# The scales of each batch come from a scratch in DRAM instead of four transposes and a copy

## The chip, the cores and the metric

The kernel runs on one core of one Trainium2 chip. The metric is the device time of one execution in microseconds; the median of three runs of the kernel before is 964.22 us (964.22 to 965.14). The core has TensorE (PE) for matrix products, VectorE (DVE), ScalarE (ACT), GpSimd (POOL), and SyncE (SP), which here issues every DMA.

## What is computed

The input x has 4 batches of 1024 rows of 512. Two layers follow one another, both steered by a vector of 128 numbers per batch (`cond`). Cut to what matters here:

```python
# layer 0, per batch b
scale = cond @ norm_w.T + 1.0                       # (4, 512): a row of 512 scales per batch
h = x * (scale[:, None, :] * rsqrt(mean(x*x) + EPS))
val, gate = split(h @ up_w.T)                       # 512 -> 2 * 2048
h = val * gelu(gate)
y = act_quant(h) @ weight_quant(down_w).T + x
# layer 1, per batch: down and up projection (512 -> 128 -> 512), weights = base + 0.1 * delta(cond)
out = y + relu(y @ Wd_b.T + bd) @ Wu_b.T + bu
```

The `(4, 512)` array `scale` is what the change moves about.

## The kernel before, in words

Each engine runs its own program, and semaphores order them. The 4096 rows are worked in 8 chunks of 512 rows (c = 0 to 7, two per batch), each chunk in 16 steps (j = 0 to 15). In step j PE makes the gate and the value products of one slice of 128 features: 12 matmuls each into a bank of PSUM (`up_products`, L1003 to L1005, f16 in three parts), with ACT's gelu (L565) and DVE's product (L851) behind them. Chunk 0 also prepares the up weights: step j loads (`load_up`), squares on ACT (`w_square`, L524), scales on DVE (`w_exponents`, `w_scale`, L688), transposes on PE (`turn_w`, L980) and splits (ACT `w_hi_half`, L530; DVE `w_lo_half`, L695) the weights that later steps use.

x of the next chunk is prepared during the current one. SP loads it (`load_x`, L277), ACT squares it (`square_x`, L498), POOL makes the reciprocal root, DVE multiplies it by that and by the row of scales (`scale_x`, L713), ACT and DVE split it in two f16 parts, and DMA transposes bring it to the layout that PE wants. For chunk 1 the squares stand in steps 0 and 1 of chunk 0, and `scale_x` in steps 5 and 6; for later chunks in steps 2 to 5 and 8 to 11 of the chunk ahead.

The scales lie on the chip as `sc`, 128 partitions by 4 x 4 (feature k * 128 + p on partition p). `scale_x` needs them along the free axis and the same on all partitions, in `sc_row` (128 x 512). Once a batch this row is made so: PE transposes four broadcast columns of `sc` into the bank TA (`spread_row`, L983 to L987), and ACT copies TA to `sc_row` (`copy_row`, L512 to L516). `row_in` puts both in step 4 of chunk 0 (batch 0) and in step 2 of chunks 1, 3 and 5 (batches 1 to 3). TA is shared with other uses, whose turns are counted by `ta_full` and `ta_freed`.

SP's order is written out by hand: setup loads, `load_up(0)` to `load_up(3)`, the broadcast of bu (L421), `load_x(1)` (L277), then chunk by chunk in `run`. Each `load_up(j)` from 3 on waits until PE has turned the weights whose buffer it takes.

Of the kernel before, what the change touches and what calls it, by code (L numbers as in the profile page):

```python
# [5 lines left out]
F32 = mybir.dt.float32  # L6
# [9 lines left out]
P = 128  # L16
# [7 lines left out]
def conditioned_block(nc, x, cond, norm_w, up_w, down_w, Wd, bd, Wu, bu, Wdd, bdd, Wdu, bdu, out):  # L24
# [15 lines left out]
    xt = x.rearrange("b l d -> (b l) d")  # L40
    ot = out.rearrange("b l d -> (b l) d")
    x1_dram = nc.dram_tensor("x1_scratch", (N, D), F32, kind="Internal").ap()
    delta_dram = nc.dram_tensor("delta_scratch", (GROUPS, P, 512), F32, kind="Internal").ap()
    delta_of = delta_dram.rearrange("g (t q b) (y k m) -> y b (g t) k q m", t=4, q=8, b=NB, y=2, k=2)

# [3 lines left out]
    with ExitStack() as ctx:  # L49
# [3 lines left out]
        def sem(name):  # L53
            return ctx.enter_context(nc.semaphore(name))
# [87 lines left out]
        def piece(p):  # L142
            o = 3072 + (p % 2) * 512
            return qreg[:, o:o + 512]
# [13 lines left out]
        def x_bank(k):  # L158
# [25 lines left out]
        piece_in = [sem(f"piece_in{i}") for i in range(2)]  # L184
        piece_biased, piece_quant, mean_step, base_done = (sem(n) for n in (
            "piece_biased", "piece_quant", "mean_step", "base_done"))
        x0_in = [sem(f"x0_in{t}") for t in range(TT)]
        x_in, x_squared, ms_done, x_rstd, x_scaled = sem("x_in"), sem("x_squared"), sem("ms_done"), sem("x_rstd"), sem("x_scaled")
        ta_full, ta_freed, x_hi_done, x_lo_done, x_turned = (sem(n) for n in (
# [22 lines left out]


        TA_BASE = KD
        TA_SC = TA_BASE + 2
        TA_MEAN = TA_SC + 1
        TA_PIECE = TA_MEAN + 1
        TA0 = TA_PIECE + FT // 2

# [11 lines left out]
            return [t for t, a in enumerate((7, 7, 8, 8) if is_first(c) else (10, 11, 12, 13)) if a == j]  # L231

        def row_in(c, j):
            return c + 1 < NCH and ((is_first(c) and j == 4) or (c % 2 == 1 and j == 2))

        def ta_row(b):
            return TA0 + b - 1 if b else TA_SC

        def mean_slot(c):
            return 1 if is_first(c) else 5  # L240
# [1 line left out]
        def is_first(c):  # L242
            return c == 0
# [27 lines left out]
        def _(sp):  # L271
# [26 lines left out]
            def load_pieces(i):  # L298
                for p in (2 * i, 2 * i + 1):
                    if i == 0 and p == 0:  # L300
                        sp.wait_ge(ta_full, TA_BASE + 2)
                    if i > 0:
                        sp.wait_ge(piece_quant, 4 * (i - 1) + 3 + p % 2)
                    dt, fb = p // 4, p % 4
                    sp.dma_start(piece(p), down_w[dt * P:(dt + 1) * P, fb * 512:(fb + 1) * 512]).then_inc(piece_in[p % 2], 16)

            def load_nat(u):
                m, t = u // 4, u % 4
# [52 lines left out]
            def run(c, par, b):  # L361
                first, last = is_first(c), b is None
                for j in range(FT):
                    if first and j < FT - 4:
                        load_up(j + 4)
                    if not last and not first and j == 1:
                        load_x(c + 1)
                    if not last:
                        for t in turns_in(c, j):
                            turn_x(c + 1, t)  # L370
                    if last and j == 4:
                        sp.wait_ge(x_turned, 32 * TT * c)
                        load_x1(0)
                        sp.wait_ge(val_full, FT * c)
                        load_x1(1)
                    if first and j == 4:
                        load_rows(3)
                        load_pieces(0)
                    if first and 7 <= j < 14:
                        load_pieces(j - 6)  # L380
                    if first and j == 11:
                        for u in range(NAT):
                            load_nat(u)
                    for u in units_at(c, j):
                        if u + NAT < UNITS:
                            load_nat(u + NAT)
                    if not first:
                        if j in (7, 8):
                            load_xr(c - 1, j - 7)
                        if 10 <= j < 10 + TT:  # L390
                            store_x1(c - 1, j - 10)
                        if j in (11, 12):
                            load_xr(c - 1, j - 9)
                    for m in batch_at(c, j):
                        if m % 2 == 1:
                            store_stage(m)
                    if last and j == 6:
                        load_deltas()
# [19 lines left out]
            load_rows(1)  # L418
            load_rows(2)
            load_up(3)  # L420
            sp.dma_start(bu_bc[:, :], bu.rearrange("(a d) -> a d", a=1).to_broadcast([P, D])).then_inc(bu_in, 16)  # L421
            load_x(1)
            chunks(run)
# [67 lines left out]
        def _(act):  # L491
# [17 lines left out]
                    act.wait_ge(x_turned, 32 * TT * (n - 1))  # L509
                act.activation(xn_hi[:, t, :], xn[:, t, :], ACT.Copy).then_inc(x_hi_done, 1)  # L510

            def copy_row(b):  # L512
                act.wait_ge(ta_full, ta_row(b) + 1)
                if b > 0:
                    act.wait_ge(x_scaled, TT * 2 * b)
                act.activation(sc_row[:, :], TA[:, :], ACT.Copy).then_inc(ta_freed, 1)  # L516

            def w_square(jj):
                act.wait_ge(upn_in[jj % 3], 32 * (jj // 3 + 1))
                for i in range(2):  # L520
# [35 lines left out]
            def run(c, par, b):  # L556
                first, last = is_first(c), b is None
                for j in range(FT):
                    n = FT * c + j
                    act.wait_ge(gate_full, n + 1)  # L560
                    if first:
                        act.wait_ge(desc_done, max(1, j - 1))
                    if not (first and j < 2):
                        act.wait_ge(max_done, n - 1)
                    act.activation(g[:, j % 2, :], GATE[j % 2][:, :], ACT.Gelu,  # L565
                                   scale=desc[:, 2 * j + 1:2 * j + 2]).then_inc(gelu_done, 1)
                    if first and j + 2 < FT:
                        w_hi_half(j + 2)
                    if first and j + 3 < FT:
                        w_square(j + 3)  # L570
                    if not first and j == 0:
                        copy_scales(c - 1)
                    if not first and j < 8:
                        round_pair(c - 1, 2 * j)
                    act.wait_ge(h_done, n + 1)
                    act.activation(g[:, j % 2, :], h[:, j, :], ACT.Abs).then_inc(abs_done, 1)  # L576
                    if not last:
                        for t in squares_in(c, j):
                            square_x(c + 1, 1 - par, t)
                        if row_in(c, j):  # L580
                            copy_row(b)
                        for t in scalings_in(c, j):
                            x_high(c + 1, t)
                    if first and 7 <= j < 15:
                        for p in (2 * (j - 7), 2 * (j - 7) + 1):
                            act.wait_ge(piece_in[p % 2], 16 * (p // 2 + 1))
                            if p == 0:
                                act.wait_ge(mean_step, 3)
                            act.activation(piece(p), piece(p), ACT.Copy, scale=wtot[:, 2:3], bias=ROUND).then_inc(piece_biased, 1)
                    if first and j >= 8:  # L590
                        copy_pieces(j - 8)
                    if first and j < 6:
                        for m in {4: (4, 5), 5: (6, 7)}.get(j, (j,)):
                            act.wait_ge(rows_in[m // 2], 16)
                            half = down_rows(m // 2)[:, FF // 2 * (m % 2):FF // 2 * (m % 2 + 1)]
                            act.activation(half, half, ACT.Abs, accum_out=wabs[:, m:m + 1]).then_inc(rows_summed, 1)
                    for m in batch_at(c, j):
                        if m % 2 == 1:
                            read_sums(m)
# [67 lines left out]
        def _(dve):  # L667
# [41 lines left out]
            def scale_x(n, t, b):  # L709
                if t == 0:  # L710
                    dve.wait_ge(x_rstd, n + 1)
                    dve.wait_ge(ta_freed, ta_row(b) + 1)
                dve.scalar_tensor_tensor(xn[:, t, :], xn[:, t, :], rstd[:, t:t + 1], sc_row[:, :],  # L713
                                         ALU.mult, ALU.mult).then_inc(x_scaled, 1)

# [252 lines left out]
        def _(pe):  # L968
# [11 lines left out]
                        mm = pe.transpose(w_bank(jj)[i][:, k * P:(k + 1) * P], upn(jj, i)[:, k * P:(k + 1) * P], identf[:, :])  # L980
                    mm.then_inc(w_turned, 1)

            def spread_row(b):  # L983
                pe.wait_ge(ta_freed, ta_row(b))
                for k in range(KD):
                    mm = pe.transpose(TA[:, k * P:(k + 1) * P], sc[:, k, b:b + 1].to_broadcast([P, P]), identf[:, :])
                mm.then_inc(ta_full, 1)  # L987

            def turn_pieces(i):
                pe.wait_ge(piece_quant, 4 * i + 4)  # L990
                pe.wait_ge(ta_freed, TA_PIECE + i)
# [78 lines left out]
            def run(c, par, b):  # L1070
# [5 lines left out]
                for j in range(FT):  # L1076
# [29 lines left out]
                    up_products(par, j, VAL[j % 2], val_full)  # L1106
                    if not first and j == 0:
                        spread_scales(c - 1)
                    if row_in(c, j):
                        spread_row(b)  # L1110
                    if first and j >= 8:
                        turn_pieces(j - 8)
                    if not first and 9 <= j < 9 + TT:
# [143 lines left out]
```

## Time and profile before

| what | value |
|---|---|
| median of 3 runs | 964.22 us |
| profiled execution: time, span | 964.68 us, 962.8 us |
| granted TensorE clock over the span | 0.995 of full speed |
| PE busy | 945.7 us (98%) |
| DVE busy | 690.6 us (72%) |
| ACT busy | 435.6 us (45%) |
| SP's DMA queue | 48.6% of 16 DMA engines, mean 147 GB/s |

The span runs from the first to the last instruction of the profiled execution; 1.9 us of its time lie outside. Matmuls overlap in their pipeline, so one of PE's durations is longer than its step to the next start, and what an instruction costs on PE is read from the distance of the starts.

### The profile page before, as it was taken

The numbers are of one execution on the slowest core, as the hardware profiler recorded it, in microseconds if no ns is written. First come the engines' busy times: TensorE is split into PE (matmuls) and PEld (weight loads), VectorE is DVE, ScalarE is ACT, GpSimd is POOL, SyncE is SP. The second block draws the span as 40 slices with busy tenths as digits, with TensorE's granted clock in tenths as the row PEclk, the third lists the DMA queues.
The fourth block names the chain that finished last, engine by engine and source line by source line (L and its number), as shares of the span: only waits on it lengthen the run. The fifth ranks groups of instructions, "written<-read, shape, count | busy, mean of one in ns | idle before, by whom it ended". The sixth has DMA issues, their size and how long they took to land.

```text
span 962.8 us, 13718 instructions
## 1 busy us (share of the span) xinstructions
PE 945.7 (98%) x5296; PEld 467.1 (49%) x5296; DVE 690.6 (72%) x1095; ACT 435.6 (45%) x801; POOL 52.7 (5%) x52
## 2 busy tenths in 40 slices
PE   7999999999999999999999999999999999999997
PEld 5555544444444444444444444444444444445585
DVE  5869887875877677866877587866977675256665
ACT  4878757322751257322752156312742256214343
POOL 1000000000000000000000000000000000000564
PEclk9999999999999999999999999999999999999999
DMA  9446543464435642564536743574436641320584
GB/s 331 150 137 165 174 160 99 142 183 124 153 122 154 175 132 98 151 177 122 164 110 164 168 146 92 154 182 118 148 112 182 167 138 55 94 77 23 183 298 175
DMA packets 103770, 141.95 MB, mean 147 GB/s; under 512 B 35732, under 2 KB 41368, under 8 KB 103192
## 3 DMA queue, kind: packets, MB, share of 16 engines
q1 hardware_dynamic: 103704, 141.06, 48.6%
q8 instruction: 42, 0.69, 0.3%
q14 instruction: 24, 0.20, 0.1%
HBM read 112.72 MB, written 20.97 MB: 139 GB/s over the span
## 4 chain that ended last, share of the span: by engine, by line
PE 95%; DVE 2%; ACT 1%; issue 1%; DMA 1%; SPq 0%; DVEq 0%; ACTq 0%
PE bank L1003 23%; PE bank L1004 22%; PE bank L1005 22%; PE bank L1056 10%; PE bank L1015 6%; PE bank L1066 1%; PE bank L980 1%; PE bank L1181 1%; PE bank L1173 1%; PE bank L1212 1%; PE bank L1202 1%; PE bank L1204 1%; PE bank L1213 1%; PE bank L1203 1%; PE bank L1194 1%
## 5 line engine op out<-in xcount | busy, mean ns | idle before, releaser
L1003 PE MATMUL bank<-x_split,w_hi 128*128 128x512 f16 x1024 | 389.4, 380 | 2.3 <-DVE x_split L706 2.3
L1004 PE MATMUL bank<-x_split,w_hi 128*128 128x512 f16 x1024 | 389.0, 380 | 0.0
L1005 PE MATMUL bank<-x_split,w_lo 128*128 128x512 f16 x1024 | 388.8, 380 | 0.0
L754 DVE STREAM_TRANSPOSE delta_reg<-delta_reg 128x512 f32<-128x512 f32 x256 | 261.2, 1111 | 13.1 <-PE bank L1015 13.1
L576 ACT ACTIVATE g<-h 128x512 f32<-128x512 f32 x128 | 80.7, 630 | 272.5 <-DVE h L851 272.5
L851 DVE SCALAR_TENSOR_TENSOR h<-bank,desc,g 128x512 f32<-128x512 f32 x128 | 94.7, 740 | 106.1 <-issue 78.2
L1003 PEld LDWEIGHTS bank<-x_split,w_hi 128*128 128x128 f16 x1024 | 100.5, 98 | 128.0 <-issue 10.6
L565 ACT ACTIVATE g<-bank,desc 128x512 f32<-128x512 f32 x128 | 87.6, 685 | 164.1 <-PE bank L1005 163.9
L1005 PEld LDWEIGHTS bank<-x_split,w_lo 128*128 128x128 f16 x1024 | 100.4, 98 | 121.4 <-issue 1.1
L1004 PEld LDWEIGHTS bank<-x_split,w_hi 128*128 128x128 f16 x1024 | 100.3, 98 | 112.6 <-issue 0.8
L1056 PE MATMUL bank<-wqT,qreg 128*128 128x512 fp8e4 x448 | 101.3, 379 | 0.0
L764 DVE TENSOR_TENSOR absrun<-absrun,g 128x512 f32<-128x512 f32 x120 | 82.5, 687 | 24.5 <-ACT g L576 23.6
L736 DVE TENSOR_TENSOR h<-h,s_bc 128x512 f32<-128x512 f32 x112 | 71.9, 684 | 2.0 <-ACT s_bc L549 2.0
L806 DVE SCALAR_TENSOR_TENSOR xr<-bank,fy,xr 128x512 f32<-128x512 f32 x30 | 22.4, 750 | 66.4 <-DMA xr<-in_x 29.4
L1056 PEld LDWEIGHTS bank<-wqT,qreg 128*128 128x128 bf16 x448 | 43.8, 98 | 52.9
L542 ACT ACTIVATE h<-h 128x512 f32<-128x512 f32 x112 | 64.4, 622 | 5.3 <-DVE h L736 5.3
L545 ACT ACTIVATE qreg<-h 128x512 bf16<-128x512 f32 x112 | 63.6, 616 | 0.0
L1015 PE MATMUL bank<-delta_reg,cond_diag 128*32 128x256 f32 x1024 | 61.9, 382 | 0.0
L464 POOL TENSOR_TENSOR rstd<-ss,mhalf 128x4 f32<-128x4 f32 x8 | 10.7, 1335 | 691.3 <-DVE ss L700 691.3
L1015 PEld LDWEIGHTS bank<-delta_reg,cond_diag 128*32 128x32 f32 x1024 | 30.0, 109 | 30.0 <-issue 13.6
L695 DVE TENSOR_TENSOR w_lo<-bank,w_hi 128x512 f16<-128x512 f32 x32 | 20.6, 685 | 12.1 <-ACT w_hi L530 12.1
L524 ACT ACTIVATE xr<-qreg 128x512 f32<-128x512 f32 x32 | 20.3, 635 | 2.8 <-DMA qreg<-in_L_cond_up_w 2.2
(164 smaller groups left out, 622.3 us busy)
## 6 DMA issues: line engine op xcount, KB each, us to landing
delta_reg<-in_L_cond_Wdd SPq DMA_DIRECT2D x64, 512.0 KB, 3.7
delta_reg<-in_L_cond_Wdu SPq DMA_DIRECT2D x64, 512.0 KB, 3.7
qreg<-in_L_cond_up_w SPq DMA_DIRECT2D x32, 256.0 KB, 4.4
xr<-in_x SPq DMA_DIRECT2D x30, 256.0 KB, 4.0
x_scratch<-xr SPq DMA_DIRECT2D x30, 256.0 KB, 4.5
xn<-in_x SPq DMA_DIRECT2D x7, 1024.0 KB, 6.3
h<-in_L_cond_down_w SPq DMA_DIRECT2D x4, 1024.0 KB, 7.8
qreg<-in_L_cond_down_w SPq DMA_DIRECT2D x16, 256.0 KB, 3.7
```

What stands on the lines that cost most here:

```text
L542: act.activation(h[:, k, :], h[:, k, :], ACT.Copy, bias=ROUND).then_inc(round_added, 1)
L565: act.activation(g[:, j % 2, :], GATE[j % 2][:, :], ACT.Gelu, scale=desc[:, 2 * j + 1:2 * j + 2]).then_inc(gelu_done, 1)
L576: act.activation(g[:, j % 2, :], h[:, j, :], ACT.Abs).then_inc(abs_done, 1)
L736: dve.tensor_tensor(h[:, k, :], h[:, k, :], s_bc[:, :], ALU.mult).then_inc(h_scaled, 1)
L754: last = dve.transpose(natT[:, t, kk, :, :].rearrange("p a (r e) -> p e a r", e=4), nat[:, u % NAT, kk, :])
L764: dve.tensor_tensor(absrun[:, :], absrun[:, :], g[:, j % 2, :], ALU.max).then_inc(max_done, 1)
L851: dve.scalar_tensor_tensor(h[:, j, :], VAL[j % 2][:, :], desc[:, 2 * j:2 * j + 1], g[:, j % 2, :], ALU.mult, ALU.mult).then_inc(h_done, 1)
L1003: pe.matmul(bank[:, :], w_hi[:, k, cols], xh[:, par, k, :], start=(k == 0), stop=False)
L1004: pe.matmul(bank[:, :], w_hi[:, k, cols], xl[:, par, k, :], start=False, stop=False)
L1005: mm = pe.matmul(bank[:, :], w_lo[:, k, cols], xh[:, par, k, :], start=False, stop=(k == KD - 1))
L1015: mm = pe.matmul(HY[32 * t:32 * t + 32, cols], cond_diag[:, a, :], natT[:, (4 * m + t) % NATT, :, a, :], start=(a == 0), stop=(a == HB - 1))
L1056: mm = pe.matmul(Y[:, :], q[:, f, t * P:(t + 1) * P], wqT[:, f, :], start=(f == 0), stop=(f == FT - 1))
```

## The change

The row of scales no longer passes through PE and ACT. In the setup SP writes `sc` to a scratch of 4 x 512 words in DRAM, in four DMAs (one per group of 128 features), each with 128 partitions by 4 single words. Once a batch SP reads one row of 512 words from the scratch, repeated for all 128 partitions, into `sc_row`. The four writes stand between `load_up(3)` and the broadcast of bu; the reads stand in step 3 of chunks 0, 1, 3 and 5. `scale_x` waits for the read in place of the copy, and the turn of TA for the row is gone.

```diff
+    sc_dram = nc.dram_tensor("sc_scratch", (NB, D), F32, kind="Internal").ap()
...
-        TA_SC = TA_BASE + 2
-        TA_MEAN = TA_SC + 1
+        TA_MEAN = TA_BASE + 2
...
         def row_in(c, j):
-            return c + 1 < NCH and ((is_first(c) and j == 4) or (c % 2 == 1 and j == 2))
+            return c + 1 < NCH and ((is_first(c) and j == 3) or (c % 2 == 1 and j == 3))
...
+            def load_row(b):
+                if b == 0:
+                    sp.wait_ge(sc_stored, 16 * KD)
+                else:
+                    sp.wait_ge(x_scaled, TT * 2 * b)
+                sp.dma_start(sc_row[:, :], sc_dram[b:b + 1, :].to_broadcast([P, D])).then_inc(sc_row_in, 16)
...
+                    if row_in(c, j):
+                        load_row(b)
...
             load_up(3)
+            sp.wait_ge(setup_dve, 9)
+            with nc.allow_non_contiguous_dma(reason="2048 words, once"):
+                for k in range(KD):
+                    sp.dma_start(sc_dram[:, k * P:(k + 1) * P].rearrange("b p -> p b"), sc[:, k, :]).then_inc(sc_stored, 16)
             sp.dma_start(bu_bc[:, :], ...)
             load_x(1)
...
-            def copy_row(b):
-                act.wait_ge(ta_full, ta_row(b) + 1)
-                if b > 0:
-                    act.wait_ge(x_scaled, TT * 2 * b)
-                act.activation(sc_row[:, :], TA[:, :], ACT.Copy).then_inc(ta_freed, 1)
...
                 if t == 0:
                     dve.wait_ge(x_rstd, n + 1)
-                    dve.wait_ge(ta_freed, ta_row(b) + 1)
+                    dve.wait_ge(sc_row_in, 16 * (b + 1))
...
-            def spread_row(b):
-                pe.wait_ge(ta_freed, ta_row(b))
-                for k in range(KD):
-                    mm = pe.transpose(TA[:, k * P:(k + 1) * P], sc[:, k, b:b + 1].to_broadcast([P, P]), identf[:, :])
-                mm.then_inc(ta_full, 1)
```

On SP, at the end of the setup, the order before was the following (L291 is `load_up`, L421 the broadcast of bu, L277 `load_x(1)`):

```order
L291 DMA qreg<-in_L_cond_up_w 128x512 x2
L421 DMA bu_bc<-in_L_cond_bu 128x512
L277 DMA xn<-in_x 128x4x512
L291 DMA qreg<-in_L_cond_up_w 128x512 x10
L296 DMA h<-in_L_cond_down_w 128x2048
```

The same place of SP's program now (L289 is `load_up`, L431 the writes to the scratch, L275 `load_x(1)`, L310 the read of the row of batch 0):

```order
L289 DMA qreg<-in_L_cond_up_w 128x512 x2
L431 DMA sc_scratch<-sc 128x4x1 x4
L432 DMA bu_bc<-in_L_cond_bu 128x512
L275 DMA xn<-in_x 128x4x512
L289 DMA qreg<-in_L_cond_up_w 128x512 x8
L310 DMA sc_row<-sc_scratch 128x512
L289 DMA qreg<-in_L_cond_up_w 128x512 x2
L294 DMA h<-in_L_cond_down_w 128x2048
```

Four DMAs of single words have moved in ahead of `load_x(1)`, and the read of the row stands four weight tiles later, behind `load_up(7)`.

On PE, in step 4 of chunk 0, the last value products, the transposes of the row (L986) and the first gate products of step 5 stood so:

```order
L1003 MATMUL bank<-x_split,w_hi 128x512
L1004 MATMUL bank<-x_split,w_hi 128x512
L1005 MATMUL bank<-x_split,w_lo 128x512
L986 MATMUL bank<-identf,sc 128x128 x4
L1003 MATMUL bank<-x_split,w_hi 128x512
L1004 MATMUL bank<-x_split,w_hi 128x512
```

The same place now, where L1000 to L1002 are the same three products:

```order
L1000 MATMUL bank<-x_split,w_hi 128x512
L1001 MATMUL bank<-x_split,w_hi 128x512
L1002 MATMUL bank<-x_split,w_lo 128x512
L1000 MATMUL bank<-x_split,w_hi 128x512
L1001 MATMUL bank<-x_split,w_hi 128x512
```

The products now follow one another; nothing else on PE is moved.

## Rows read from the trace of the kernel before

**Rows 1.** The page: busy time by engine, and the chain that ended last

```profile
PE 945.7 (98%) x5296; PEld 467.1 (49%) x5296; DVE 690.6 (72%) x1095; ACT 435.6 (45%) x801; POOL 52.7 (5%) x52
PE 95%; DVE 2%; ACT 1%; issue 1%; DMA 1%; SPq 0%; DVEq 0%; ACTq 0%
```

**Rows 2.** Timeline of PE in chunk 0: start, us, engine line op out<-in

```profile
51.93 0.38 PE L1005 MATMUL bank<-x_split,w_lo 128*128 128x512 f16 x1
52.15 0.60 PE L986 MATMUL bank<-identf,sc 128*128 128x128 f32 x4
52.58 0.38 PE L1003 MATMUL bank<-x_split,w_hi 128*128 128x512 f16 x1
...
67.06 0.38 PE L1005 MATMUL bank<-x_split,w_lo 128*128 128x512 f16 x1
69.74 1.97 PE L980 MATMUL bank<-identf,qreg 128*128 128x128 f32 x8 [2.30 <-DVE qreg L688]
```

**Rows 3.** Stretches: PE, PEld, DVE, ACT, POOL busy, granted clock, DMA share, GB/s

```profile
65.00:70.00 5.00, 2.70 (x13) 1.15 (x12) 3.43 (x12) 3.88 (x10) 0.00 (x0) 0.95 0.14 33
70.00:75.00 5.00, 5.00 (x23) 3.15 (x23) 4.80 (x12) 4.10 (x9) 0.00 (x0) 0.71 0.19 39
355.00:365.00 10.00, 10.00 (x51) 4.78 (x49) 9.31 (x13) 7.06 (x15) 0.00 (x0) 1.00 0.34 106
```

**Rows 4.** Instructions of L986 and of L516: duration ns min/median/max, first and last start

```profile
L986 PE MATMUL bank<-identf,sc x16: 272/273/273, 52.1 to 575.6; 128*128 128x128 f32 x16
...
L516 ACT ACTIVATE sc_row<-bank x4: 575/577/582, 53.7 to 577.5; 128x512 f32<-128x512 f32 x4
```

**Rows 5.** The chain in order of time, 55 to 75 us

```profile
58.37 0.22 PE bank L1004
58.89 0.75 DVE h L851
```

**Rows 6.** L277: us from issue to landing, min/median/max

```profile
DMA to landing us min/median/max: 5.8/6.3/9.9
```

**Rows 7.** Timeline of DVE: steps 1 and 5 of chunk 0

```profile
32.08 1.29 DVE L695 TENSOR_TENSOR w_lo<-bank,w_hi 128x512 f16<-128x512 f32 x2 [0.81 <-ACT w_hi L530]
33.38 0.75 DVE L851 SCALAR_TENSOR_TENSOR h<-bank,desc,g 128x512 f32<-128x512 f32 x1
34.92 0.88 DVE L688 TENSOR_SCALAR qreg<-qreg,winv 128x512 f32<-128x512 f32 x2
...
61.23 1.41 DVE L713 SCALAR_TENSOR_TENSOR xn<-xn,rstd,sc_row 128x512 f32<-128x512 f32 x2
```

**Rows 8.** Timeline of SP, setup: issues, their start and duration

```profile
9.87 2.80 SPq L417 DMA_DIRECT2D bdc<-in_L_cond_bd  x1
12.71 0.91 SPq L296 DMA_DIRECT2D h<-in_L_cond_down_w  x2
...
17.65 0.43 SPq L277 DMA_DIRECT2D xn<-in_x  x1
```

**Rows 9.** DMA in 14.9:15.9, in 22:27 and in 17:30

```profile
DMA packets 604, 0.35 MB, mean 349 GB/s; under 512 B 21, under 2 KB 571, under 8 KB 604
DMA packets 1004, 1.94 MB, mean 387 GB/s; under 512 B 69, under 2 KB 69, under 8 KB 1002
DMA  9999999999999998999999999999999999999521
```

**Rows 10.** Timeline of ACT, steps 0 and 1 of chunk 0

```profile
28.10 0.63 ACT L576 ACTIVATE g<-h 128x512 f32<-128x512 f32 x1 [0.74 <-DVE h L851]
28.64 0.61 ACT L498 ACTIVATE x_split<-xn 128x512 bf16<-128x512 f32 x1
30.90 0.67 ACT L565 ACTIVATE g<-bank,desc 128x512 f32<-128x512 f32 x1
31.47 1.06 ACT L530 ACTIVATE w_hi<-bank 128x512 f16<-128x512 f32 x2
```

**Rows 11.** Timeline of PE, step 2 of chunk 0

```profile
36.14 1.04 PE L980 MATMUL bank<-identf,qreg 128*128 128x128 f32 x8
```

More of the change, by code:

```diff
@@ L186, in conditioned_block @@
             "piece_biased", "piece_quant", "mean_step", "base_done"))
+        sc_stored, sc_row_in = sem("sc_stored"), sem("sc_row_in")
         x0_in = [sem(f"x0_in{t}") for t in range(TT)]
@@ L233, in row_in @@
         def row_in(c, j):
-            return c + 1 < NCH and ((is_first(c) and j == 4) or (c % 2 == 1 and j == 2))
-        def ta_row(b):
-            return TA0 + b - 1 if b else TA_SC
+            return c + 1 < NCH and ((is_first(c) and j == 3) or (c % 2 == 1 and j == 3))
         def mean_slot(c):
@@ L579, in run @@
                             square_x(c + 1, 1 - par, t)
-                        if row_in(c, j):
-                            copy_row(b)
                         for t in scalings_in(c, j):
@@ L1108, in run @@
                         spread_scales(c - 1)
-                    if row_in(c, j):
-                        spread_row(b)
                     if first and j >= 8:
```

## Prediction

> **What bounds the kernel now.** I read the page's busy times and chain first, then PE's timeline at the removed transposes, then what the new DMAs move: the timelines of SP, ACT, DVE and PE over the first 40 us. PE is busy for 98% of the span and makes 95% of the chain [rows 1], so what leaves PE's queue leaves the time one for one, and what makes PE wait adds one for one. DVE and ACT matter only where PE waits for them, which after the setup is in chunk 0, where they also prepare the weights. The largest such wait there is at 67 us: PE stands for 2.30 us before the weight transposes at 69.74 [rows 2], and the granted clock then falls to 0.71 on average in the next 5 us, a stretch partly at the lower of the two levels, 1.2 GHz [rows 3]. Remember that pair; it gives the price of any stall of that length.
>
> **What is removed.** Sixteen transposes on PE, four per batch [rows 4]. Their durations overlap, so I take the distance of starts: the first of four starts at 52.15, the next matmul at 52.58, 0.43 us later, and the matmul ahead of them stands at 51.93, its usual 0.22 us before [rows 2]. No wait is mixed in. The other three fours have the same duration each (272 to 273 ns) and stand in stretches in which PE is never idle, as the one around the third shows [rows 3]. 4 x 0.43 = 1.7 us leave PE, all on the path.
>
> Four copies of 0.577 us leave ACT [rows 4]. Three stand in chunks where ACT is busy for 7.06 of 10 us and PE waits for nobody [rows 3]: worth nothing. The one of batch 0, at 53.7, stands some 5 us ahead of the chain that ends in the stall at 67 us. In that chain DVE's product starts at 58.89 and the chain comes to it from PE [rows 5], so an earlier ACT does not help by itself; PE is 0.43 us earlier and the chain moves with it. The stall keeps its length and the 1.7 us stand. The wait for a turn of TA goes too; PE never stood at it.
>
> **What is added after the setup.** Four reads of 256 KB. DMA share is 0.34 in such a stretch [rows 3] and each read is used five steps after its issue in chunks 1, 3 and 5 (a step is 962.8 us / 128 = 7.5 us on average, against 6.3 us for a load of 1 MB [rows 6]). SP loses about 0.45 us at each. The first is issued behind `load_up(7)`, near 38 us, and used at 61.23 [rows 7]. All hidden; the cover fails only if the writes to the scratch have not landed by about 50 us, since SP would then stand in front of `load_up(8)`. So four reads: 0.
>
> **What is added in the setup.** Four writes of 128 x 4 words, 512 pieces of 4 bytes each, 2048 in all, or 128 per DMA engine; with one semaphore update for each DMA 132. Their data are ready when SP gets there. They stand ahead of the broadcast of bu and of `load_x(1)`, issued at 17.65 [rows 8], 9.9 us to landing, the longest of its kind [rows 6], so it lands at 27.55. The DMA engines are saturated from 17 us to 29 us [rows 9], so SP's delay is at first free (the queue has work), but the engines' time for 2048 pieces is not.
>
> No row shows a 4-byte write to DRAM. From below: nothing but the four issues, 0.43 us each [rows 8], all inside the backlog, 0 us. From the rows of small reads: with pieces of mostly 512 B, 604 packets take 1 us of 16 engines, 26 ns each; with pieces of mostly 2 KB, 1004 take 5 us, 80 ns each [rows 9]. 132 x 26 ns = 3.4 us; 132 x 80 ns = 10.6 us as the upper end. A 4-byte piece carries far less than 512 B, so I take two thirds of the nearer price, about 2.2 us, and keep 0 and 10.6 us.
>
> The load of x then lands by either of two limits. Queue: 27.55 + 2.2 = 29.8. Issue: the four writes put 2112 more pieces in a queue that already held SP at its issues (2.80 us for one of 128 words, against 0.43 [rows 8]), so SP probably comes past them only when the queue has reached them. Before, it reached the 1 MB of x at 27.55 less 1.05 MB / 387 GB/s = 24.8 us, and the 256 KB of bu ahead of it at 24.1. I estimate that `load_x(1)` is issued near 24 us instead of 17.65; with the shortest landing time, 5.8 us [rows 6], that is 29.8 too. I take 29.9.
>
> Who waits: ACT's first square of chunk 1 starts at 28.64, directly behind its L576 [rows 10]. Behind it in ACT's queue are another square, a sum of the down weights, gelu of step 1 (30.90), the upper halves of weight tile 3 (31.47) and the squares of tile 4. None of these shows idle time ahead [rows 10], so a late landing moves them all. DVE's `w_lo` at 32.08 waits for ACT, its product at 33.38 follows at once, and the scaling of tile 4 starts at 34.92 [rows 7] and ends its first half near 35.4. PE turns this half at 36.14 [rows 11]: slack about 0.75 us. So PE stands by (landing - 28.64 - 0.75) = landing - 29.4. At 29.9 this is 0.5 us. Until step 5 ACT and DVE find their lost time again, since their idle gaps in steps 2 to 4 are waits for PE.
>
> The sum: -1.7 + 0.5 = -1.2 us. Against the profiled execution, 964.68 us, that is 963.5; the profiled run stands 0.46 us above the median of the runs, 964.22, so against the median I get 963.0 us.
>
> The Trainium skill has a rule against this change: in "DMA: Bandwidth & Descriptors", section "Rules for kernel authors", a strided last dimension becomes one descriptor per element, and its "Specifications" say that below 512 B the DMA engine does a read-modify-write. The only single-word DMA here is a read (the issue of 2.80 us), so no run shows the second; if it doubles the price of each piece, the rival below is the outcome.
>
> **The rivals.** (0.2% of this kernel is 1.9 us, about what a measurement can tell from no change.)
>
> A. All hidden: the writes cost the engines under about 1.5 us and x lands before 29.4. Then the full 1.7 us stay: 962.5. For it: 4 bytes are almost nothing, and the queue is backlogged anyway. Against it: the shortest landing after a late issue is already 29.8. Even this is 0.18%, just inside no change.
>
> B. Late x, slower. If x(1) lands after about 31.7 us, PE stands for over 2.3 us at the transposes of 36.14, as long as the stall after which the clock fell [rows 2], and what follows runs at the lower level. In the stretch 70 to 75 the clock was 0.71, so 0.29 x 5 = 1.45 us were missing, and about 0.2 us in the stretch before: 1.7 us. Two ways lead here. The pieces could be dear: at 80 ns, x lands at 27.55 + 10.6 = 38.2, PE stands for 8.8 us, with the clock 10.5, less 1.7: +8.8 us, 973.0. Or SP could be held at each write as it was at the one DMA of single words, 2.80 us against 0.43 us for `load_x(1)` with its 512 pieces of 2 KB [rows 8]: 4 x 2.8 = 11.2, issue at 28.8, landing at 34.6, PE stands 5.2 us, with the clock 6.9, less 1.7: +5.2 us, 969.4. For it: that row. Against it: at 9.87 over a dozen loads had been issued and the engines were far behind, so the hold may be the queue's and not the words'. Yet the two issues from 12.71 on took 0.46 us each [rows 8] soon after, so the doubt stays. Were the hold proportional to the number of pieces, 11.2 us for each write, the loss would be over 35 us; I give that 3 in 100. The point from which B decides is a PE stall of 3.7 us with the clock included.
>
> C. The gain is more than PE's time: ACT's 0.5 us at 53.7 shortens the stall at 67 us, and the lower clock goes with it. That would give -1.7 - 1.7 = -3.4 or better, about 961. Against it: the chain is released by PE at 58.89 [rows 5].
>
> **How the numbers follow.** My forecast (part of the gain given back, landing between 29.4 and 31.5): 0.35. A: 0.25. B: 0.35. C: 0.05. The forecast and A lie within 0.2% nearly whole; of A I give 0.1 to the faster side, since 1.7 and 1.9 us are hardly apart, and C adds 0.05. So faster 0.15, within 0.2% 0.49, slower 0.36. The likeliest case's own range is 962.4 to 964.7. The range reaches down past A to 962.1 and up into B past the issue price, to 971.0; beyond it lie C and B's dear end.
>
> **What would show it.** PE: 16 transposes fewer, and the value products of step 4 followed by the gate products of step 5 at 0.22 us. SP: the duration of the four writes, and the start of `load_x(1)` (near 24 us). ACT: the start of the first square of chunk 1 (near 29.9 in place of 28.64). PE at the transposes of step 2: a wait near 0.5 us that was not there. PE's stall at 67 us: 2.3 us as before. The granted clock of 35 to 40 us at 1.00 would speak against B. The forecast is wrong if ACT's square starts before 29.4 or after 31.5, if the stall at 67 us changes its length, or if DVE's `scale_x` waits for a row.

## The result

The changed kernel takes 974.13 us (median of 5 runs, 973.27 to 974.73) against 965.14 us of the kernel before in the same runs: a ratio of 1.0096, 95% interval 1.0085 to 1.0107, or 9.0 us slower. Forecast were 963.0 us and a range up to 971.0. The size of the outcome is that of rival B's dear end, for which the prediction had worked out +8.8 us (973.0 against 964.22).

The page of the changed kernel: span, busy time, and the chain by engine.

```profile
span 972.2 us, 13687 instructions
PE 946.9 (97%) x5280; PEld 466.5 (48%) x5280; DVE 690.9 (71%) x1095; ACT 433.9 (45%) x797; POOL 52.7 (5%) x52
PE 92%; DVE 2%; DMA 2%; ACT 1%; SPq 1%; issue 1%; DVEq 0%; ACTq 0%
```

PE has 16 matmuls fewer, and yet its busy time is above that of [rows 1]: part of its work was done at the lower clock level. DMA's share of the chain has gone from 1% to 2%. This is the piece of the chain behind that, in order of time (start, us, what):

```profile
24.32 13.71 DMA xn<-in_x
38.02 0.02 issue
38.05 0.04 ACT x_split L509
```

The timeline of SP (L431 the four writes, L432 the broadcast of bu, L275 `load_x(1)`) answers to [rows 8]:

```profile
17.52 4.07 SPq L431 DMA_DIRECT2D sc_scratch<-sc  x4
21.63 2.64 SPq L432 DMA_DIRECT2D bu_bc<-in_L_cond_bu  x1
24.32 0.43 SPq L275 DMA_DIRECT2D xn<-in_x  x1
24.79 22.79 SPq L289 DMA_DIRECT2D qreg<-in_L_cond_up_w  x8
47.63 0.43 SPq L310 DMA_DIRECT2D sc_row<-sc_scratch  x1
```

The load of x is issued at 24.32, where the prediction had it. What it had not is the landing, 13.7 us later. Between 22 and 32 us the mean busy share of the DMA engines and what they moved were, in 40 slices of 0.25 us:

```profile
DMA  9999999999990000060003131122204002994412
GB/s 393 377 377 265 178 98 56 29 3 1 1 0 0 0 0 0 0 66 0 0 0 33 16 8 8 0 25 16 8 8 25 0 8 16 106 25 16 16 8 25
```

The words go by between 22.5 and 24.5 us (2070 packets under 512 B), and then the engines move next to nothing, 14 GB/s from 24 to 32 us against 264 in the kernel before, although the 256 KB of bu and the 1 MB of x, from 24.79 us on also the next weight tile, are there to be moved. In the kernel before the same stretch is saturated until 29 us [rows 9]. ACT feels it twice (timeline; in brackets the idle time ahead and what ended it):

```profile
29.06 0.63 ACT L529 ACTIVATE xr<-qreg 128x512 f32<-128x512 f32 x1 [2.66 <-DMA qreg<-in_L_cond_up_w]
...
38.05 0.63 ACT L509 ACTIVATE x_split<-xn 128x512 bf16<-128x512 f32 x1 [6.99 <-DMA xn<-in_x]
```

The first is weight tile 3, which was issued ahead of the writes; its second half took 12.0 us from issue to landing, against 7.4 in the kernel before. The second is the first square of chunk 1, 28.64 before [rows 10]. On PE, the waits of chunk 0 (timeline, only rows with idle time):

```profile
31.99 1.09 PE L983 MATMUL bank<-identf,qreg 128*128 128x128 f32 x8 [1.77 <-DVE qreg L691]
44.78 1.97 PE L983 MATMUL bank<-identf,qreg 128*128 128x128 f32 x8 [6.09 <-DVE qreg L691]
80.31 1.97 PE L983 MATMUL bank<-identf,qreg 128*128 128x128 f32 x8 [2.30 <-DVE qreg L691]
```

The last is the stall of [rows 2], with the same length. The second is the one at step 2, whose transposes stood at 36.14 [rows 11]. The clock in the stretches around it (columns as in [rows 3]):

```profile
40.00:45.00 5.00, 0.22 (x1) 0.22 (x2) 3.39 (x11) 4.81 (x13) 0.00 (x0) 0.77 0.11 42
45.00:50.00 5.00, 5.00 (x18) 2.79 (x18) 2.78 (x6) 4.25 (x11) 1.39 (x1) 0.55 0.39 129
```

PE comes back to a clock of 0.55, mostly the lower level of 1.2 GHz, and loses (1 - 0.55) x 5 = 2.25 us. The whole, against the span before: waits 1.77 + 6.09 = 7.9, clock 2.25, transposes -1.7, and PE's first product 0.35 us later (18.97 in place of 18.62, a wait of the same 2.32 us in both): 8.8 of the 9.4 us between the spans. Of the other 0.6 us, some 0.25 are the clock between 20 and 25 us (0.78 against 0.83); the rest is not assigned.

What was removed went as planned. The products of steps 4 and 5 now follow at 0.22 us:

```profile
62.93 0.38 PE L1002 MATMUL bank<-x_split,w_lo 128*128 128x512 f16 x1
63.14 0.38 PE L1000 MATMUL bank<-x_split,w_hi 128*128 128x512 f16 x1
```

DVE's 28 instructions with the row of scales wait for no row. The packets of the page, 106457 against 103770, are 2687 more: 2048 words with 64 semaphore updates and four reads of 128 rows with 64 updates would be 2688. So the writes did go as single words, as the Trainium skill says of a strided last dimension in "DMA: Bandwidth & Descriptors", "Rules for kernel authors".

### The profile page after: what moved, and what is told of

Read it like the earlier page. It is cut to its first block, busy times and chain, and to the rows that moved or that the text cites. A ratio compares the mean times of both kernels' runs of the same rounds, so it can differ in the third digit from the quotient of the medians.

```text
span 972.2 us, 13687 instructions
## 1 busy us (share of the span) xinstructions
PE 946.9 (97%) x5280; PEld 466.5 (48%) x5280; DVE 690.9 (71%) x1095; ACT 433.9 (45%) x797; POOL 52.7 (5%) x52
## 2 busy tenths in 40 slices
DMA packets 106457, 142.99 MB, mean 147 GB/s; under 512 B 37908, under 2 KB 43544, under 8 KB 105880
## 4 chain that ended last, share of the span: by engine, by line
PE 92%; DVE 2%; DMA 2%; ACT 1%; SPq 1%; issue 1%; DVEq 0%; ACTq 0%
PE bank L1000 22%; PE bank L1001 22%; PE bank L1002 22%; PE bank L1053 10%; PE bank L1012 6%; DMA xn<-in_x 2%; PE bank L1063 1%; PE bank L983 1%; PE bank L1189 1%; PE bank L1176 1%; PE bank L1168 1%; PE bank L1207 1%; PE bank L1197 1%; PE bank L1199 1%; PE bank L1208 1%
## 5 line engine op out<-in xcount | busy, mean ns | idle before, releaser
L1000 PE MATMUL bank<-x_split,w_hi 128*128 128x512 f16 x1024 | 390.1, 381 | 2.3 <-DVE x_split L709 2.3
L1002 PE MATMUL bank<-x_split,w_lo 128*128 128x512 f16 x1024 | 389.4, 380 | 0.0
L1000 PEld LDWEIGHTS bank<-x_split,w_hi 128*128 128x128 f16 x1024 | 100.6, 98 | 128.8 <-issue 11.3
L1002 PEld LDWEIGHTS bank<-x_split,w_lo 128*128 128x128 f16 x1024 | 100.5, 98 | 121.8 <-issue 1.9
L767 DVE TENSOR_TENSOR absrun<-absrun,g 128x512 f32<-128x512 f32 x120 | 82.6, 688 | 24.5 <-ACT g L581 23.6
L475 POOL TENSOR_TENSOR rstd<-ss,mhalf 128x4 f32<-128x4 f32 x8 | 10.7, 1335 | 700.6 <-DVE ss L703 700.6
L983 PE MATMUL bank<-identf,qreg 128*128 128x128 f32 x128 | 18.3, 292 | 10.2 <-DVE qreg L691 10.2
```

The source lines that it names most:

```text
L767: dve.tensor_tensor(absrun[:, :], absrun[:, :], g[:, j % 2, :], ALU.max).then_inc(max_done, 1)
L1000: pe.matmul(bank[:, :], w_hi[:, k, cols], xh[:, par, k, :], start=(k == 0), stop=False)
L1002: mm = pe.matmul(bank[:, :], w_lo[:, k, cols], xh[:, par, k, :], start=False, stop=(k == KD - 1))
```

## The experiments

Theory 1: the whole loss is in the four writes of single words. Theory 2: it is in the later issue of the load of x. Theory 3: it is in the reads of the rows or the new wait. All ratios are to the kernel before, run beside.

**rows_only.** The writes are left out, and the reads fetch rows of x, so the scales are missing from the computation.

```diff
-            sp.wait_ge(setup_dve, 9)
-            ... (the four writes)
...
-                sp.dma_start(sc_row[:, :], sc_dram[b:b + 1, :].to_broadcast([P, D])).then_inc(sc_row_in, 16)
+                sp.dma_start(sc_row[:, :], xt[b:b + 1, :].to_broadcast([P, D])).then_inc(sc_row_in, 16)
```

> The changed kernel without the four writes to the scratch; the four reads fetch a row of x in place of a row of scales, so the scales are left out of the computation. Theory 1 (all of the loss is in the four writes of single words): what is left is the gain of 16 transposes, 1.7 us under the kernel before, 0.998 of its time. Theory 2 (SP's late issue of the load of x): the same here, since nothing holds SP. Theory 3 (the reads of the rows or the new wait cost something): the time stays above the kernel before, up to 9 us.

963.25 us, ratio 0.9977 (0.9968 to 0.9986). Theory 3 falls. The gain of the rest is there: the interval is 1.4 to 3.1 us, and the 1.7 us from the starts on PE lie inside it.

**before_writes.** The opposite: the kernel before with the writes alone.

```diff
             load_up(3)
+            sp.wait_ge(setup_dve, 9)
+            with nc.allow_non_contiguous_dma(reason="2048 words, once"):
+                for k in range(KD):
+                    sp.dma_start(sc_dram[:, k * P:(k + 1) * P].rearrange("b p -> p b"), sc[:, k, :]).then_inc(sc_stored, 16)
             sp.dma_start(bu_bc[:, :], ...)
```

> The kernel before with nothing but the four writes of single words added at the place of the change; nobody reads them. Theory 1: the full loss, 9.0 + 1.7 = 10.7 us over the kernel before, about 1.011; DMA share near nothing from 25 to 30 us and x landing near 38 us. Theory 2: the same time, since the issue is late here too. Theory 3: under 2 us.

975.43 us, ratio 1.0103 (1.0089 to 1.0116), 10.3 us by the medians. ACT's first square of chunk 1 stands at 38.45, PE waits 7.24 us at step 2. Theory 1's sum closes within the intervals: 10.3 - 1.7 = 8.6 against the 9.0 measured for the whole change. Theory 3, under 2 us, falls here too.

**writes_behind_x.** The same four writes behind `load_x(1)`.

```diff
-            ... (the wait and the four writes)
             sp.dma_start(bu_bc[:, :], ...)
             load_x(1)
+            ... (the wait and the four writes)
```

> The changed kernel with the four writes issued behind the load of x in place of ahead of it. Theory 1 (the pieces themselves are dear, about 70 ns each on their engine, and hold whatever is in flight or queued): x may land at 27.6 to 30 if it is done before the engines reach the writes, but weight tile 4, issued behind them and needed near 32.4, lands near 37, so some 3 to 7 us of loss stay. Theory 2 (the late issue of x): x lands at 27.6, and the time falls to 1.7 us under the kernel before.

970.67 us, ratio 1.0055 (1.0041 to 1.0069). Theory 2 falls as the cause of the whole loss: x is issued at 17.88, as before, and still lands 14.8 us later, near 32.7. Yet the order is worth something: this kernel stands 5.3 us above the kernel before where the changed one stands 9.0 above it, some 4 us less. How much of these is the earlier issue of x and how much that the words are no longer ahead of it in the queue, no run separates. First what the trace says of the loads of `load_x` in this kernel:

```profile
DMA to landing us min/median/max: 5.9/6.8/14.8
```

And ACT's timeline at the first square of chunk 1 and at the next late weight tile:

```profile
32.68 0.63 ACT L509 ACTIVATE x_split<-xn 128x512 bf16<-128x512 f32 x1 [3.94 <-DMA xn<-in_x]
37.93 0.63 ACT L529 ACTIVATE xr<-qreg 128x512 f32<-128x512 f32 x1 [1.34 <-DMA qreg<-in_L_cond_up_w]
```

A load that stands ahead of the words in SP's order lands 5 us late (14.8 us from issue to landing against 9.9). I had allowed for "27.6 to 30"; the writes reach further ahead than that.

**writes_late.** The changed kernel with the writes in step 2 of chunk 0.

```diff
+                    if first and j == 2:
+                        store_scales()      # the wait and the four writes
...
-            ... (the wait and the four writes, ahead of bu)
```

> The changed kernel with the four writes in step 2 of chunk 0, behind weight tile 6, where the DMA engines were busy for a third of the time, in place of the setup. Theory 1 (the stall of some 8 us costs only what is in flight or queued around it): x and tile 3 land as in the kernel before. Tile 6, issued just ahead of the writes near 31 us, may land up to 8 us late, near 43, and is squared near 44; so the time is 1.5 to 2 us under the kernel before, as rows_only, or a few tenths more. Theory 2 (the writes as such cost the kernel time wherever they stand): over 5 us above.

963.37 us, ratio 0.9987 (0.9978 to 0.9996). The four writes take 2.37 us of SP at 31.02 and land in up to 10.7 us, and PE, after two waits of 0.27 and 0.58 us in its first 5 us of work, waits for nothing but the known stall, 2.30 us, which ends at 69.14. The engines stall here too: the second half of the weight tile issued just ahead of the writes takes 11.6 us from issue to landing (3.0 in the kernel before) and from 34 to 42 us they move 13 GB/s. But ACT squares that tile only at 44.22, without a wait. The same writes cost 10 us in one place and nothing that can be told from zero in another: a full gain of 1.7 us would be 0.9982, inside the interval.

**What makes the words dear.** Six kernels, each the kernel before with one kind of small transfer at the place of the change. What differs from before_writes is each time the inner line, and in the first two the range of k:

```diff
 one_write      for k in range(1): as before_writes
 write_of_128   for k in range(1): sp.dma_start(sc_dram[0:1, 0:P].rearrange("b p -> p b"), sc[:, 0, 0:1])
 words_apart    sc_dram (NB, D, 128): sp.dma_start(sc_dram[:, k * P:(k + 1) * P, 0].rearrange("b p -> p b"), sc[:, k, :])
 words_64_apart sc_dram (NB, D, 16): the same line
 pieces_of_16   sc_dram (KD, P, NB): sp.dma_start(sc_dram[k, :, :], sc[:, k, :])
 words_read     sp.dma_start(sc_back[:, k, :], xt[0:NB, k * P:(k + 1) * P].rearrange("b p -> p b"))
```

> The kernel before plus one of the four writes (512 words). Theory 1a: a quarter of the stall, about 2 us, x lands near 29.6, and PE waits 0 to 0.5 us: within 1 us of the kernel before. A fixed price for the first write that follows loads: 8 us or more over.

> The kernel before plus the four writes of single words, as in before_writes (10.3 us over the kernel before), but each word to a place of its own, 512 B from the next, in a scratch of 1 MB. Theory 1a (each small write has its price wherever it goes, about 4 ns of the memory for each of 2048): again 9 to 11 us over. Theory 1b (the price is that 2048 writes meet in the same 8 KB): the stall of the DMA engines is gone or under 2 us, and the time within 1 us of the kernel before.

> The kernel before plus four writes of the same 8 KB into a scratch laid out as the chip has it, so that each partition writes 16 bytes in one piece: 512 pieces in place of 2048. Theory 1a: a quarter of the stall, some 2 us, of which most is within the slack: 0 to 2 us over the kernel before. Theory 1b: pieces of neighbours still meet in the same 8 KB; also a quarter or less. If the price goes by bytes, as before_writes: 10 us.

> The kernel before plus four reads of 512 single words of x from DRAM to the chip at the same place of SP's program, into a buffer that nobody uses. Theory 1 (it is the write to DRAM that is dear): 132 pieces per engine at 9 to 26 ns, 1.2 to 3.4 us of the engines, x lands by 31, and the time is 0 to 2 us over the kernel before. Theory 4 (any piece of 4 bytes is dear): 10 us over, as before_writes.

> The kernel before plus one write of 128 single words to 512 neighbouring bytes. Theory 1c (writes to one stretch of 512 B or less wait for one another at some 60 ns each, and different stretches go side by side; one_write and before_writes stalled equally long with 128 words per stretch): the stall is as long as with 512 words, and the time about 5 us over the kernel before. Theory 1a (a price per word): a sixteenth of the stall, no change within 1 us.

> The kernel before plus the four writes of single words, each word 64 B from the next, so 8 words per stretch of 512 B. Theory 1c: little is left of the neighbours' waiting, the stall is no longer than with words 512 B apart, and the time is 6 us over the kernel before or less. If what counts is that the words lie within a few KB of one another, it lies between words_apart (6.4 us over) and before_writes (10.3 us over).

The table's third column is the ratio with its interval; the fourth is where x is issued, the fifth what the second half of weight tile 3, issued ahead of the small pieces, took from issue to landing, the sixth where ACT's first square of chunk 1 starts, all in us.

| kernel | small pieces | ratio (95%) | issue of x | tile 3 | first square | GB/s in 24 to 32 us |
|---|---|---|---|---|---|---|
| before | none | 1 | 17.65 | 7.4 | 28.64 | 264 |
| before_writes | 2048 words written into 8 KB | 1.0103 (1.0089 to 1.0116) | 23.94 | 11.4 | 38.45 | 15 |
| one_write | 512 words into four stretches of 512 B | 1.0062 (1.0042 to 1.0082) | 19.22 | 12.0 | 33.66 | 129 |
| write_of_128 | 128 words into 512 B | 1.0059 (1.0043 to 1.0074) | 17.95 | 13.5 | 33.84 | 164 |
| words_apart | 2048 words, 512 B apart | 1.0066 (1.0051 to 1.0081) | 24.03 | 8.4 | 33.17 | 167 |
| words_64_apart | 2048 words, 64 B apart | 1.0062 (1.0048 to 1.0076) | 24.12 | 9.1 | 33.07 | 164 |
| words_read | 2048 words read | 1.0034 (1.0023 to 1.0045) | 24.36 | 8.9 | 31.22 | 253 |
| pieces_of_16 | 512 pieces of 16 B into 8 KB | 1.0007 (0.9997 to 1.0016) | 19.87 | 8.8 | 29.42 | 270 |

The profiled executions do not start alike: PE's first product of chunk 0 stands between 17.77 (words_read) and 19.65 (one_write), against 18.62 before. So the starts in the table compare only to about 1 us; the ratios and the times from issue to landing do not have this fault.

Theory 1a, a price per word, falls: 128 words cost as much as 512. So does 1b in its plain form: words with places of their own still cost 6.4 us (by the ratio). What fits the rows is that two things add up. Words that meet in the same few hundred bytes hold one another and what is in flight beside them: 128 words into 512 B delay x by 5 us and tile 3, issued ahead, by 6. Words 512 B or 64 B apart delay tile 3 by 1.0 and 1.7 us only. And a large number of words costs time wherever it goes (2048 words, 512 B or 64 B apart, delay x by 4.5 us alike). Together, in before_writes, they delay x by 9.8 us. My theory 1c was right for the times of write_of_128 and words_64_apart; its "60 ns each" no run shows. Read words cost a third of what words written in the same pattern do, so it is not the 4 bytes alone.

That these are two things and not one is argued from the sizes, not shown; how the memory does this, and on what unit the meeting goes, no run here shows. Two more points stay open. The kernels with 2048 words also issue x some 6 us later, and a load issued at 24 us lands at 29.8 at the earliest, by the shortest time of 5.8 us [rows 6]. So part of what the large number costs, and most of it for words_read (6.8 us from issue to landing), may be the late issue. And pieces_of_16 changes two things at once, the size of a piece and how many meet in 512 B (32 in place of 128); which of them makes it cheap was not tried.

The smallest of them, write_of_128, in 22 to 32 us (slices as above):

```profile
DMA  9999999999992292593125793939858984896699
GB/s 377 352 393 385 361 378 394 410 377 295 164 66 98 98 98 98 107 107 57 66 82 123 188 156 139 131 147 139 172 164 205 238 180 172 213 213 197 197 320 229
```

For some 7 us after one DMA of 512 bytes the engines move little more than a third of the 385 GB/s of the kernel before. From 25 to 30 us they count as busy for 0.75 of the time (their packets are under way) and move 131 GB/s; in one_write it is 0.96 and 96 GB/s. Their busy share says little here of what they get done. A weight tile issued ahead of this DMA and x behind it pay for that (ACT's timeline in the same kernel):

```profile
30.02 0.63 ACT L531 ACTIVATE xr<-qreg 128x512 f32<-128x512 f32 x1 [5.14 <-DMA qreg<-in_L_cond_up_w]
...
33.84 0.63 ACT L505 ACTIVATE x_split<-xn 128x512 bf16<-128x512 f32 x1 [1.82 <-DMA xn<-in_x]
```

**turned_once.** A way into the scratch without small pieces; each row is then read as four pieces of 512 B per partition.

```diff
+            pe.transpose(VAL[1][0:NB * KD, 0:P], sc[:, :, :].rearrange("p k b -> p (k b)"), identf[:, :])   # once, ahead of chunk 0
+            act.activation(sc_t[:, :], VAL[1][0:NB * KD, 0:P], ACT.Copy)
...
             load_x(1)
+            sp.dma_start(sc_dram[:, :], sc_t[:, :])                   # 16 rows of 512 B, scratch laid out (k b) p
-            ... (the wait and the four writes; new waits and the changed read are left out here)
```

> The whole change with another way into the scratch: PE turns the 128 x 16 scales once in its idle time before chunk 0, ACT copies 16 rows of 128 words, and one DMA behind the load of x writes them in 16 pieces of 512 B; each batch's row is read in 4 pieces of 512 B per partition. Theory 1: 0.4 us of PE at most in idle time, so about 1.5 us under the kernel before, 0.998 to 0.999; the stall at the transposes of step 2 is gone. Theory 2: the same, since the load of x is issued at 17.7 again. Theory 3: no better than the changed kernel less a few tenths.

963.11 us, ratio 0.9978 (0.9970 to 0.9987): 2.1 us under the kernel before, and level with rows_only (0.9977), which has no writes at all. Its transpose stands in PE's wait ahead of chunk 0, and the wait ends about where it did (18.62 before):

```profile
16.26 0.27 PE L1154 MATMUL bank<-identf,sc 128*16 128x128 f32 x1
18.74 0.58 PE L1004 MATMUL bank<-x_split,w_hi 128*128 128x512 f16 x1 [2.21 <-DVE x_split L712]
```

Between 22 and 32 us its DMA engines are busy as in the kernel before:

```profile
DMA  9999999999999999999999999998531100000003
```

## Why the prediction was wrong

- **The 16 transposes, -1.7 us.** Right: rows_only is 1.9 us faster by the medians, with 1.7 inside the interval.
- **The four copies on ACT and the waits at TA, 0.** Right; the stall after step 6 kept its 2.30 us. Rival C did not come.
- **The four reads of the row, 0.** Right: DVE waits for no row in any kernel that reads one.
- **The four writes, "about 2.2 us" of the engines, kept between 0 and 10.6.** This is the step that failed. I took the busy time of a 512 B packet and cut it by a share of my own ("two thirds of the nearer price") because a word carries less. The form of the term was wrong too: a price per piece that the engines work off. The runs show no such price (128 words cost 0.59%, 512 words 0.62%). The words went by in about 2 us, and then the engines moved 14 GB/s for 8 us. That x landed at 38.0, close to the upper end of 27.55 + 10.6 = 38.2, is luck: that end was worked out as engines busy with 132 pieces at the price of 2 KB packets, while from 25 to 30 us they were busy for 0.15 of the time.
- **The landing by "either of two limits".** The issue near 24 us was right (24.32). The second limit, 5.8 us from issue to landing, took for granted that the queue was free by then. It took 13.7. And the queue limit took for granted that what is ahead of the words is safe: tile 3 (PE waits 1.77 us) and, in writes_behind_x, x itself show that it is not.
- **Who waits, landing less 29.4.** Right for the place where the chain meets PE: 38.0 gives 8.6 us, and the transposes of step 2 start at 44.78 in place of 36.14, 8.6 us later. The wait there is only 6.09, because PE was already late by the 1.77 of tile 3, a wait that the prediction did not have, and by its later start.
- **The clock, 1.7 us for a long stall.** Right in kind, 2.25 measured.
- **Rival B** had the size (+8.8 against +9.0 measured) with a chance of 0.35, but by a price per piece that the runs do not show; its agreement is in part luck, as said above. Its second way, SP held for 2.8 us at each write, did not come: the four took 4.07 us. The weight went wrong with the one unknown: the rows that the forecast leaned on were of reads, and words_read shows that reads of words cost a third as much. The Trainium skill's sentence on transfers below 512 B ("DMA: Bandwidth & Descriptors", "Specifications") spoke for the dear price. The runs agree for written words (1.0103, and 1.0034 for read ones), but not for pieces of 16 B, which are below 512 B as well and cost 1.0007. That a read-modify-write is behind the price, no run shows.

## What to carry to other kernels

Look at the pieces of a layout change through DRAM. As single words it cost some 10 us here; with the data turned on the chip first, so that the write has rows of 512 B, nothing that could be seen. Or put it where nothing that was issued near it is awaited soon, as in writes_late. Do not price a small write by its bytes or its count, and look at the loads ahead of it in the queue as well as behind. An unknown with ends of 0 and 10 us is not settled by picking a value near the cheap end; here one run of the kernel before with the writes alone would have settled it.

## What was not expected of the hardware

One DMA that writes 128 words of 4 bytes into 512 bytes of DRAM, beside loads under way, lowered what the DMA engines moved from 264 to 164 GB/s over 8 us, stretched half a weight tile issued ahead of it from 7.4 to 13.5 us between issue and landing, and cost the kernel 0.59% (0.43% to 0.74%). Four times as many words at their own four stretches cost no more. The same 8 KB in pieces of 16 B cost 0.07%, which is not clear of zero.
